# The y products of an AdaLN-FFN kernel: from one 128-row matmul with a block-diagonal table to two 64-row matmuls

## The reference, cut to what matters

```python
# x: (64, 64, 1024); weights: (16, 64, 64); condition: (64,)
W = weights[condition]
y = jnp.einsum('bct,bcd->bdt', x, W)              # per batch: 64 channels in, 64 out
base  = jnp.einsum('bsi,oi->bso', y, W_org)       # 1024 x 1024
q = jnp.einsum('bi,ki->bk', y.mean(axis=1), Wq)
scores = jnp.einsum('bk,ek->be', q, lora_keys) / math.sqrt(K)
coeffs = jax.nn.softmax(scores, axis=-1)
h = jnp.einsum('bsi,eir->bser', y, lora_down)     # 8 experts, rank 64
delta = jnp.einsum('be,bser,ero->bso', coeffs, h, lora_up)
out = x + base + delta
```

## Time and profile before

| | |
|---|---|
| median of 3 runs | 760.37 us |
| the profiled execution | 759.43 us, of it 757.6 us from the first to the last instruction (the span) |
| TensorE matmuls (PE) busy | 710.0 us, 94% of the span |
| weight loads (PEld) busy | 594.4 us, 78% |
| VectorE, ScalarE, GpSimd busy | 489.7, 239.2, 127.4 us |
| matmul records of y (L1179) | 512 in 32 steps of 16 |
| mean granted TensorE clock | 0.982 of full speed |

### The profile page before, as it was taken

One profiled execution on the slowest core, in us unless ns is written; L12 is line 12 of the kernel. 1 busy time (PEld: TensorE's weight loads), 2 busy tenths in 40 slices (PEclk: granted clock), 3 DMA queues, 4 the chain that ended last, 5 costly groups with the idle time before them and its releaser, 6 DMA issues.

```text
span 757.6 us, 10562 instructions
## 1 busy us (share of the span) xinstructions
PE 710.0 (94%) x3385; PEld 594.4 (78%) x3385; DVE 489.7 (65%) x785; ACT 239.2 (32%) x455; POOL 127.4 (17%) x113
## 2 busy tenths in 40 slices
PE   5878999999999999999996829999999999999996
PEld 5766888888888888888885628888888888888885
DVE  3478466465565655746546697777776767676763
ACT  4246235153361432624413540222222222222220
POOL 1630000000000000000000002333333333333332
PEclk9979999999999999999999969999999999999999
DMA  8983344443444425335221545666666666666643
GB/s 214 291 238 124 125 129 144 129 143 115 143 140 139 134 106 165 127 124 154 98 84 56 200 161 161 218 221 222 216 223 219 217 222 226 219 221 217 224 150 106
DMA packets 83672, 128.10 MB, mean 169 GB/s; under 512 B 18458, under 2 KB 51234, under 8 KB 81570
## 3 DMA queue, kind: packets, MB, share of 16 engines
q1 hardware_dynamic: 83280, 127.36, 52.5%
q10 hardware_dynamic: 338, 0.07, 0.0%
HBM read 77.07 MB, written 50.33 MB: 168 GB/s over the span
## 4 chain that ended last, share of the span: by engine, by line
PE 83%; issue 6%; DVE 5%; POOL 3%; DMA 1%; ACT 1%; SPq 0%; POOLq 0%; DVEq 0%; ACTq 0%
PE x_ps L1300 22%; PE w_ps L1300 16%; PE x_ps L1239 10%; PE h_ps L1202 10%; PE x_ps L1202 10%; PE w_ps L1239 8%; PE y_ps L1179 6%; DVE tb_l L761 1%; DVE org_f L761 1%; PE y_ps L1289 1%; POOL down_l L468 1%; POOL tu_l L463 1%; DMA blkx<-in_x_dram 1%; POOL yq_l L449 1%; POOL blk L475 1%
## 5 line engine op out<-in xcount | busy, mean ns | idle before, releaser
L475 POOL TENSOR_TENSOR blk<-blk,blkx 128x512 f32<-128x512 f32 x64 | 97.6, 1525 | 325.6 <-DMA blkx<-in_x_dram 195.1
L764 DVE TENSOR_TENSOR blk<-w_ps,blk 128x512 f32<-128x512 f32 x96 | 66.0, 688 | 89.5 <-PE w_ps L1239 45.1
L1300 PE MATMUL x_ps<-tb_h,ba_h 128*128 128x512 f32 x256 | 100.8, 394 | 15.1 <-DVE blk L764 14.1
L1300 PE MATMUL x_ps<-tb_h,ba_l 128*128 128x512 f32 x256 | 100.4, 392 | 0.0
L1300 PE MATMUL x_ps<-tb_l,ba_h 128*128 128x512 f32 x256 | 100.2, 391 | 0.0
L513 ACT ACTIVATE ba_h<-bs 128x512 fp32r<-128x512 f32 x64 | 38.0, 625 | 130.8 <-DVE bs L761 130.8
L1300 PE MATMUL w_ps<-tb_h,ba_l 128*128 128x512 f32 x192 | 74.7, 389 | 0.0
L1300 PE MATMUL w_ps<-tb_l,ba_h 128*128 128x512 f32 x192 | 74.7, 389 | 0.0
L1300 PE MATMUL w_ps<-tb_h,ba_h 128*128 128x512 f32 x192 | 74.7, 389 | 0.0
L1300 PEld LDWEIGHTS x_ps<-tb_h,ba_h 128*128 128x128 f32 x256 | 48.5, 189 | 26.6 <-DVE blk L764 15.2
L764 DVE TENSOR_TENSOR blk<-x_ps,blk 128x512 f32<-128x512 f32 x64 | 42.5, 682 | 36.0 <-PE x_ps L1300 36.0
(11 more groups left out here) (97 smaller groups left out, 1380.3 us busy)
## 6 DMA issues: line engine op xcount, KB each, us to landing
x_sb<-in_x_dram SPq DMA_DIRECT2D x32, 512.0 KB, 4.0
y_dram<-y_full SPq DMA_DIRECT2D x64, 256.0 KB, 2.7
r_dram<-blk SPq DMA_DIRECT2D x64, 256.0 KB, 2.4
yb<-y_dram SPq DMA_DIRECT2D x32, 512.0 KB, 7.5
blk<-r_dram SPq DMA_DIRECT2D x16, 1024.0 KB, 6.7
blkx<-in_x_dram SPq DMA_DIRECT2D x32, 512.0 KB, 7.0
out_dram<-blk SPq DMA_DIRECT2D x64, 256.0 KB, 3.9
x_sb<-in_L_ffn_W_org_dram SPq DMA_DIRECT2D x8, 512.0 KB, 3.6
```

The costliest lines, as they stand in the source:

```text
L475: pool.tensor_tensor(blk[p % 3][:, b, :], blk[p % 3][:, b, :], blkx[:, h, n, :], ALU.add).then_inc(x_added, 1)
L764: nc.vector.tensor_tensor(dst, a, b, ALU.add).then_inc(done, 1)
L1300: mm = nc.tensor.matmul(bank, ba[s][n][:, k, :], tb[w][n][:, k, :], start=(first and k == 0 and i == 0), stop=(k == 3 and i == 2), skip_gr ...
```

## The change

Each batch's product is made for itself. `cws` and `cw_sb` lose their batch axis: the two 64 by 64 tables lie one above the other, batch 0's on partitions 0 to 63 and batch 1's on 64 to 127, with no zero blocks. `make_y(t)` now does a whole step: for each of the eight column blocks two matmuls, one for each batch, whose stationary operand is the 64 rows of x of that batch (64 by 128) and whose moving operand is its 64 by 64 table. Batch 0's results go to one PSUM bank and batch 1's to the other, so a bank now holds all eight column blocks of one batch and not four blocks of both. The copies read a bank of one batch and write it into `y_full` between the other's (`y_of_batch`). Everything that reads `y_full`, and TensorE where it takes a bank pair again, now waits until both banks of a step are copied (`wait_y`).

```diff
-        cw_sb = small("cw_sb", [P, 4, BT, C])
-        cws = small("cws", [P, 3, BT, 2, C // 2])
+        cw_sb = small("cw_sb", [P, 4, C])
+        cws = small("cws", [P, 3, 2, C // 2])
...
+        def wait_y(engine, t):
+            if t >= 4:
+                engine.wait_ge(y_copied, 2 * t - 2)
+            else:
+                engine.wait_ge(y_copied, t + 1)
+                engine.wait_ge(y_copied_dve, t + 1)
+        def y_bank(t):
+            return (y_ps, x_ps, w_ps)[t % 3] if t < 4 else y_ps
+        def y_of_batch(t, b):
+            return y_full[:, 2 * (t % 4):2 * (t % 4) + 2, :, :].rearrange("p r k (b d) -> p (r k) b d", b=BT)[:, :, b, :]
...
-                pool.tensor_copy(cws[:, t % 3, :, :, :],
-                                 cw_sb[:, i, :, :].rearrange("p b (d h) -> p b h d", h=2)).then_inc(cw_ready, 1)
+                pool.tensor_copy(cws[:, t % 3, :, :],
+                                 cw_sb[:, i, :].rearrange("p (d h) -> p h d", h=2)).then_inc(cw_ready, 1)
...
             def copy_y(n):
-                t, r = n // 2, n % 2
+                t, b = n // 2, n % 2
                 act.wait_ge(y_done, n + 1)
-                if n >= 8:
-                    act.wait_ge(y_summed, max(n - 7, 8))
-                    act.wait_ge(y_lo[r], t - 3)
-                    act.wait_ge(y_stored[n % 8], 16 * (n // 8))
-                copy(y_full[:, n % 8, :, :], y_bank(n).rearrange("p (k n) -> p k n", k=4), y_copied)
+                if t >= 4:
+                    act.wait_ge(y_summed, max(2 * t - 6, 8))
+                    for r in range(2):
+                        act.wait_ge(y_lo[r], t - 3)
+                        act.wait_ge(y_stored[(2 * t + r) % 8], 16 * (t // 4))
+                copy(y_of_batch(t, b), y_bank(t)[:, b, :].rearrange("p (k d) -> p k d", k=KC), y_copied)
...
-            def make_y(n):
-                t, r = n // 2, n % 2
+            def make_y(t):
                 i = t % 4
                 pe.wait_ge(x_loaded[i], 16 * (t // 4 + 1))
                 pe.wait_ge(cw_ready, t + 1)
-                if n == 6:
-                    pe.wait_ge(*copied(0))
-                elif n == 7:
-                    pe.wait_ge(*copied(1))
-                elif n >= 8:
-                    pe.wait_ge(*copied(n - 2))
-                for k in range(4):
-                    col = (4 * r + k) * P
-                    mm = nc.tensor.matmul(y_bank(n)[:, k * P:(k + 1) * P], x_sb[:, i, col:col + P],
-                                          cws[:, t % 3, :, :, :].rearrange("p b h d -> p (b h d)"),
-                                          start=True, stop=True)
-                mm.then_inc(y_done, 1)
+                if t == 3:
+                    wait_y(pe, 0)
+                elif t >= 4:
+                    wait_y(pe, t - 1)
+                for k in range(KC):
+                    for b in range(BT):
+                        rows = slice(b * C, (b + 1) * C)
+                        mm = nc.tensor.matmul(y_bank(t)[:, b, k * C:(k + 1) * C],
+                                              x_sb[rows, i, k * P:(k + 1) * P],
+                                              cws[rows, t % 3, :, :].rearrange("p h d -> p (h d)"),
+                                              start=True, stop=True)
+                        if k == KC - 1:
+                            mm.then_inc(y_done, 1)
```

More of the change, by code:

```diff
@@ L256, in b_sum @@
             return bs[n][:, :, :].rearrange("p k (a d) -> p k a d", a=4)
-        def copied(n):
-            if n >= 8:
[L261 to L268, removed]
+        def wait_y(engine, t):
[8 more added lines that the diff above has]
+            return y_full[:, 2 * (t % 4):2 * (t % 4) + 2, :, :].rearrange("p r k (b d) -> p (r k) b d", b=BT)[:, :, b, :]
         U11, U12 = up_raw[:, 0:2, 0, :], up_raw[:, 0:2, 1, :]
@@ L294, in load_cw @@
                     which = sp.value_load(cond_sb[0:1, BT * t + b:BT * t + b + 1], min_val=0, max_val=NCOND - 1)
-                    sp.dma_start(cw_sb[b * C:(b + 1) * C, i, b, :], cond_w[which, :, :]).then_inc(cw_loaded[i], 16)
+                    sp.dma_start(cw_sb[b * C:(b + 1) * C, i, :], cond_w[which, :, :]).then_inc(cw_loaded[i], 16)
             def load_down(n):
@@ L304, in store_y @@
                 t, r = n // 2, n % 2
-                sp.wait_ge(*copied(n))
+                wait_y(sp, t)
                 sp.dma_start(y_dram[t // 2, :, 4 * r:4 * r + 4, t % 2, :],
@@ L476, in add_x @@
                                    ALU.add).then_inc(x_added, 1)
-            pool.memset(cw_sb[:, :, :, :], 0.0).then_inc(first_steps, 1)
+            pool.memset(cw_sb[:, :, :], 0.0).then_inc(first_steps, 1)
             pool.memset(ident[:, :], 0.0).then_inc(first_steps, 1)
@@ L517, in load_cw @@
                     which = act.value_load(cond_sb[0:1, BT * t + b:BT * t + b + 1], min_val=0, max_val=NCOND - 1)
-                    act.dma_start(cw_sb[b * C:(b + 1) * C, t % 4, b, :], cond_w[which, :, :]).then_inc(cw_loaded[t % 4], 16)
+                    act.dma_start(cw_sb[b * C:(b + 1) * C, t % 4, :], cond_w[which, :, :]).then_inc(cw_loaded[t % 4], 16)
             def copy_y(n):
-                t, r = n // 2, n % 2
+                t, b = n // 2, n % 2
                 act.wait_ge(y_done, n + 1)
-                if n >= 8:
-                    act.wait_ge(y_summed, max(n - 7, 8))
-                    act.wait_ge(y_lo[r], t - 3)
-                    act.wait_ge(y_stored[n % 8], 16 * (n // 8))
-                copy(y_full[:, n % 8, :, :], y_bank(n).rearrange("p (k n) -> p k n", k=4), y_copied)
+                if t >= 4:
[4 more added lines that the diff above has]
+                copy(y_of_batch(t, b), y_bank(t)[:, b, :].rearrange("p (k d) -> p k d", k=KC), y_copied)
             def split_y(n):
@@ L532, in split_y @@
                 i = t % 4
-                act.wait_ge(*copied(n))
+                wait_y(act, t)
                 if n >= 8:
@@ L766, in copy_y @@
             def copy_y(n):
+                t, b = n // 2, n % 2
                 dve.wait_ge(y_done, n + 1)
-                nc.vector.tensor_copy(y_full[:, n % 8, :, :],
-                                      y_bank(n).rearrange("p (k n) -> p k n", k=4)).then_inc(y_copied_dve, 1)
+                nc.vector.tensor_copy(y_of_batch(t, b),
+                                      y_bank(t)[:, b, :].rearrange("p (k d) -> p k d", k=KC)).then_inc(y_copied_dve, 1)
             def sum_y(n):
                 t, r = n // 2, n % 2
-                dve.wait_ge(*copied(n))
+                wait_y(dve, t)
                 if n >= 8:
@@ L1277, in turn_org @@
                 if c == 0:
-                    pe.wait_ge(*copied(2 * T - 1))
+                    wait_y(pe, T - 1)
                 else:
@@ L1346, in _ @@
             nc.tensor.transpose(keys_ps, keys_sb[:, :], ident[0:E, 0:E]).then_inc(keys_turned, 1)
-            for n in range(8):
-                make_y(n)
+            for t in range(4):
+                make_y(t)
             for q in range(NQ):
@@ L1361, in _ @@
                         if more:
-                            make_y(n + 2 * m)
-                            make_y(n + 2 * m + 1)
+                            make_y(4 * (q + 1) + m)
                         else:
```

## The result

The changed kernel takes 774.27 us (median of 4 runs, 772.77 to 777.68) against 760.17 us for the kernel before (median of the 4 runs now there): a ratio of 1.017 (95% interval 1.014 to 1.020). It is slower, but by 14 us and not by the 44 of the forecast; the range, 757 to 816, holds it, and it lies where the second rival put it (769 to 779, centre 773).

What follows compares the result with a forecast made beforehand. The prediction took TensorE to bound the kernel, with y's records bound by weight loads. Steps +40.8, start +3 and copies +0.5 summed to +44.3 us on 759.43, giving 804 us; range 757 to 816.

Steps and rivals of the forecast that it cites:

- the second rival: In y steps: row halves overlap, but changing between full and half height costs; 769 to 779 us, centre 773; chance 0.19.
- a step of y lies on the path 24 times: In the cycles after the first, 24 of 32 y steps count straight into the end; eight stand in the start.
- the nearest row: Profile row taken for 64-row loads in y: 0.106 us a record, same columns and type, records one behind the other.
- +40.8 us: Term for the 24 y steps on the path, each 1.70 us longer.
- the prediction's own sign: Prediction is wrong if a y step takes under 2.5 us or a 64-row load's distance is below 0.1 us.
- full overlap: Rival in y steps: row halves load beside each other, step stays at 1.70 us; 760 to 762 us, chance 0.19.
- the load of 8 rows: The trace's one load of few rows, 177 ns against 140 at full height; taken to show fewer rows aren't shorter.
- The copies: Copy on ScalarE before the high part for P2 starts later: 0.5 us over seven cycles, between 0 and 2.
- The start: Eight y steps up to about 69 us, where TensorE waits for others: +3 us taken, between 0 and 7.
- +6.3 for the four steps: In the start, the four first y steps add 6.8 us, moving the first h product to about 24.6, +6.3.
- the likeliest case: No overlap of the row halves' loads in y steps: 804 us, own range 798 to 811, chance 0.42.
- the five cases: No overlap 0.42; full overlap 0.19; overlap with switch costs 0.19; no overlap plus switches 0.08; faster 0.12.

Runs made afterwards that it cites:

- late: Kernel before the change, with both copies of a step beginning only at the step's end: 765.69 us, ratio 1.005.
- after_pairs: Changed kernel with the y steps in the cycles made two at a time, halving the changes of height: 775.85 us, ratio 1.017.
- quads: Changed kernel with each y matmul cut once more, into two of 64 stationary columns (four quarters of the array): 754.5 us, ratio 0.988.
- same_rows: Changed kernel with both batches' matmuls on rows 0 to 63 (half of y wrong): 875.57 us, ratio 1.147.
- the pair of extra matmuls: Kernel before the change, one more matmul heading each y step: on 64 rows 776.62 us, on 128 rows as control 770.07 us.
- batch_outer: Changed kernel with batch 0's eight matmuls of a step first, then batch 1's eight, not alternating: 842.76 us, ratio 1.109.

## Why the prediction was wrong, point by point

- What bounds the kernel, and that a step of y lies on the path 24 times: right. PE fills the cycles, but for 0.2 us in late and 0.8 in after_pairs.
- That a record of y is bound by its weight load "(or by the issue of the pair)", and that 64 moving columns save nothing by themselves: right, with the bracket ruled out by quads. The halves together still need 1.70 us, and only the cut to 64 stationary columns made the step shorter.
- The step that failed is "they follow one another as now, a step takes 32 x 0.106 = 3.40 us, 1.70 more", taken because it was "the nearest row". That row had full-height loads, all on the same rows, and so said nothing on loads in different halves. Measured: 0.053 us a record, 1.70 us for the 32, and +0.15 for the step in the chain, so that +40.8 us became +9.5 for the cycles, edges and copies included. By the prediction's own sign (a step under 2.5 us, a load's distance under 0.1) it is wrong. same_rows gives the 3.4 back, and so shows that this one property of the change kept 24 x 1.70 us off the path. The Trainium skill's rule on row groups ("TensorE: Matmul & The Clock Gate", Part 3), cited and then left at 0.19 with full overlap and 0.19 with costs, held. The runs agree with it: 1.70 us for 32 records where the halves take turns, 3.4 on one half alone; batch_outer's 3.3 adds that here the turns had to be between neighbours. Between two bounds far apart, nearness of a row was the wrong judge; the mechanism had to be asked.
- The other support of that step was weak too: the load of 8 rows, 177 ns against 140. It ran at 4.13 us, before the first step of y, whose own first full-height load took 0.29 us and later ones 0.19, so the two loads compared were most likely not at the same clock. It couldn't say that fewer rows make a load no shorter. same_rows can: its first load, of 64 rows, took 0.29 us as well, and its steps twice 1.70.
- The second rival, overlap with a price for each change of tile size, is what happened. Its price was 0.32 to 0.70 us a step; 0.36 was seen in the trace and 0.31 by the pair of extra matmuls, at its lower end and just under it. I read it as the tail of the last matmul and part of a load; no run separates the two. "TensorEngine Tiling (Array Packing)" in the Trainium skill, Key Properties, says that the change of mode drains the engine; the loads that don't run ahead at y's entry, and the 0.31 us of the pair, agree. That 774.27 fell next to this rival's centre of 773 is in part luck: the profile has 4.9 us from a stretch that the change doesn't touch.
- The copies: the place was right, the size three times the one taken, "0.5 us in all, between 0 and 2". In the changed kernel they cost 0.21 us a cycle, about 1.5 us over seven cycles, inside the bounds. By themselves (late) they cost 0.45 a cycle, about 3 us.
- The start: first h at 23.27 for the forecast 24.6, the third quarter of h at 44.23 for 45.0, the gap of 6.39 gone; net +1.4 and +3.0 in two profiles for a forecast of +3. The forecast that the clock stays at 2.4 GHz through that gap was right, but other stretches ran at 1.2: the first four steps took 3.4 us each, twice the 1.70 of the cycles, where the kernel before had come to 1.8 from the second on, and h began at 0.43 us a matmul. (In same_rows the same steps take 6.8 us, twice its 3.4: the overlap is there at both levels.) Its +6.3 for the four steps came near the measured 5.0 by luck, since it stood for loads one after another at full clock and what happened was overlap at half the clock:

```profile
6.87 3.68 PE L1184 MATMUL y_ps<-cws,x_sb 64*128 64x64 f32 x32 [2.12 <-POOL cws L462]
17.14 3.66 PE L1184 MATMUL y_ps<-cws,x_sb 64*128 64x64 f32 x32
23.27 0.77 PE L1209 MATMUL x_ps<-yq_h,down_h 128*128 128x512 f32 x1 [2.47 <-DVE yq_l L766]
44.23 0.50 PE L1209 MATMUL h_ps<-yq_h,down_h 128*128 128x512 f32 x1
```

- The direction was right, but by the edges and not by the step; the likeliest case and its size were not. That the range held the result says nothing for the mechanism, since it held three of the five cases whole.

## What to carry to other kernels

In this kernel, cutting a matmul to half the rows paid nothing where its weight load was the bound: the halves load side by side, but each has as many loads as before. It paid (1%) when the matmuls were also cut to 64 stationary columns, so that four quarters run at once. The halves overlapped only with the tiles alternating in the order of issue; for the quarters no other order was run. Each stay in another tile size costs about 0.3 us for its two ends here, so put such matmuls together, but keep something between a product and the chain of small work that waits for it.

## What the runs showed of the hardware that had not been expected

- The granted clock fell without any gap in TensorE's work. With 3.7 us stays on half the rows (same_rows) the h matmuls behind them ran at 1.2 GHz and the kernel lost 101 us against the changed one, of which the longer steps of the cycles explain 43 (24 x 1.78) and the start 25; with 1.7 us stays on both halves (the changed kernel) the windows of the cycles read 1.00.
- At the start of the changed kernel the clock was still at its half level after 13.7 us of y without a gap: four steps of 3.4 us, and the h product behind them began at 0.43 us a matmul. The kernel before had left that level by its second step. The windows still give 1.00 for that time, so there the level has to be read from the distances between instructions.
- 64 pairs of load and matmul were issued in some 0.86 us (1.09 less 0.23), 13 ns a pair, in the four quarters.
